# A spacing memset on GpSimd behind the gathers of the last sequence

## The reference

```python
x = L0_attn_x                                        # (8, 512, 128) float32
x = x + 0.5 * ffn(layernorm(x), gate_w, w1, w3, w2)  # 8 experts, each token goes to 2 of them
x = x + attn(layernorm(x), ...)                      # scan over the tokens of a sequence
x = x + 0.5 * ffn(layernorm(x), gate_w, w1, w3, w2)  # the same experts again

def ffn(x, gate_w, w1, w3, w2):
    probs = softmax(x @ gate_w)
    weights, experts = top_k(probs, 2)               # weights divided by their sum
    # out[token] = sum over its 2 experts of weight * (silu(x @ w1[e]) * (x @ w3[e])) @ w2[e]
```

## Time and profile before

| | us |
|---|---|
| time, median of 3 runs | 606.3 |
| lowest and highest of the 3 | 605.97, 606.87 |
| the profiled execution's own time | 611.62 |
| span of the profiled execution, from the first to the last instruction | 609.8 |
| PE busy in it | 525.3 |
| DVE busy | 438.5 |
| POOL busy | 398.1 |
| ACT busy | 318.7 |

### The profile page before, as it was taken

How to read it: one execution, slowest core, us unless ns; L and a number is a source line. 1 busy time by engine, 2 the same in 40 slices (tenths; PEclk the granted TensorE clock), 3 DMA queues, 4 the chain that set the end, 5 groups by cost and what they waited for, 6 DMA issues and landing times.

```text
span 609.8 us, 18683 instructions
## 1 busy us (share of the span) xinstructions
PE 525.3 (86%) x5906; PEld 480.7 (79%) x5906; DVE 438.5 (72%) x1241; ACT 318.7 (52%) x703; POOL 398.1 (65%) x500
## 2 busy tenths in 40 slices
PE   1234899999999899999989989999999999998992
PEld 1233789998977789778888779898798988998981
DVE  4871873556778998879999885887888857248742
ACT  5433574444675657576375663587456454443420
POOL 1182049499999991199954999300985997999982
PEclk9999899999999999999999998999999999999997
DMA  8963233445332221222221132210112432523322
GB/s 278 330 210 110 60 102 110 131 145 128 90 98 83 72 79 55 69 62 66 83 76 49 59 114 75 67 42 27 54 59 84 113 107 76 182 81 102 97 71 60
DMA packets 88632, 60.28 MB, mean 99 GB/s; under 512 B 10337, under 2 KB 82146, under 8 KB 88418
## 3 DMA queue, kind: packets, MB, share of 16 engines
q1 hardware_dynamic: 55586, 31.03, 17.3%
q0 software_dynamic: 8192, 16.79, 9.6%
q10 hardware_dynamic: 24768, 11.28, 6.4%
HBM read 29.69 MB, written 29.37 MB: 97 GB/s over the span
## 4 chain that ended last, share of the span: by engine, by line
PE 61%; issue 10%; ACT 9%; DVE 8%; SPq 5%; POOL 4%; DMA 1%; another core or an unknown queue 1%; DVEq 0%; ACTq 0%; POOLq 0%
PE py L1330 20%; PE pa L1316 16%; PE pb L1316 15%; PE pT L1303 3%; POOL rows_in L766 3%; PE bkB L1380 2%; ACT xn L866 2%; PE bkB L1401 2%; DVE h L1170 1%; ACT sil L847 1%; POOL pace L801 1%; SPq L664 1%; PE bkA L1380 1%; SPq L677 1%
## 5 line engine op out<-in xcount | busy, mean ns | idle before, releaser
L766 POOL DMA_INDIRECT rows_in<-parts,slot x128 | 135.2, 1057 | 179.5 <-DVE slot L1091 157.6
L1330 PE MATMUL py<-ffn_w,h 128*128 x1416 | 196.6, 282 | 9.5 <-ACT yrow L830 8.1
L1170 DVE TENSOR_TENSOR h<-sil,pb 128x512 f32<-128x512 f32 x177 | 120.8, 686 | 107.1 <-PE pb L1316 56.3
L1330 PEld LDWEIGHTS py<-ffn_w,h 128*128 128x128 f32 x1416 | 173.2, 193 | 15.1 <-issue 12.3
L1316 PE MATMUL pa<-rT,ffn_w 128*128 128x128 f16 (+1 forms) x1752 | 150.9, 232 | 18.1 <-DVE h L1170 9.8
L1316 PE MATMUL pb<-rT,ffn_w 128*128 128x128 f16 (+1 forms) x1752 | 155.8, 231 | 0.0
L1316 PEld LDWEIGHTS pa<-rT,ffn_w 128*128 x1752 | 123.3, 99 | 33.4 <-issue 21.8
L785 POOL DMA_INDIRECT yg<-rows_out,slot x120 | 121.0, 1008 | 19.4 <-issue 19.2
L801 POOL MEMSET pace<- 128x544 uint8 x232 | 133.0, 573 | 0.2
L1316 PEld LDWEIGHTS pb<-rT,ffn_w 128*128 x1752 | 122.9, 98 | 7.5 <-issue 0.2
L847 ACT ACTIVATE sil<-pa 128x512 f32<-128x512 f32 x177 | 105.4, 595 | 37.8 <-PE pa L1316 32.3
(11 more groups left out here) (167 smaller groups left out, 493.5 us busy)
## 6 DMA issues: line engine op xcount, KB each, us to landing
rows_out<-yrow ACTq DMA_DIRECT2D x162, 64.0 KB
rin<-rows_in SPq DMA_DIRECT2D x65, 128.0 KB
rows_in<-zrow SPq DMA_DIRECT2D x34, 128.0 KB
shared<-in_w SPq DMA_DIRECT2D x16, 256.0 KB, 6.8
rin<-rows_in SPq DMA_DIRECT2D x47, 64.0 KB
rows_in<-zrow SPq DMA_DIRECT2D x2, 1472.0 KB, 12.1
xres<-in_x SPq DMA_DIRECT2D x4, 512.0 KB, 5.8
ffn_w<-in_w SPq DMA_DIRECT2D x8, 256.0 KB
```

Of the source, the lines that this page charges most:

```text
L766: pool.indirect_dma_start(rows_in[g][:], bass.IndirectOffsetOnAxis(ap=slot[:, c, at:at + 1], axis=0), parts[:, at, :], None).then_inc(s_sc ...
L1170: dve.tensor_tensor(h[:, t % RING, :], sil[:, t % 2, :], pb[t % 2][:], ALU.mult).then_inc(s_h, 1)
L1330: mm = pe.matmul(py[:], h[:, step % RING, at:at + T], w, start=(c == 0), stop=(c == FC - 1))
```

## The change

The condition `t < TILES - 1` is taken away, and the loop over the last run's gathers gets the same memset behind each gather but the very last one, with the count of `sent` carried on.

```diff
@@ -796,12 +796,15 @@
                     scatter(*one)
                 else:
                     gather(*one)
-                if t < TILES - 1:
-                    wait(pool, s_pace, sent - PACES + 1)
-                    pool.memset(pace[:, sent % PACES, :], 0).then_inc(s_pace, 1)
+                wait(pool, s_pace, sent - PACES + 1)
+                pool.memset(pace[:, sent % PACES, :], 0).then_inc(s_pace, 1)
             for run in range(RUNS):
                 for one in every(run, range(UNITS[run] if PEND[run] == TILES else 0)):
                     gather(*one)
+                    sent += 1
+                    if one != (run, UNITS[run] - 1, JU - 1, TOPK - 1):
+                        wait(pool, s_pace, sent - PACES + 1)
+                        pool.memset(pace[:, sent % PACES, :], 0).then_inc(s_pace, 1)
```

## The result

The changed kernel takes 609.61 us in the median of five runs (609.04 to 609.86), the kernel before on the same chip 606.87 (605.97 to 607.89). The ratio is 1.0046, with a 95% interval of 1.0034 to 1.0059, which is 2.1 to 3.6 us slower. The forecast was 609.3 and slower. The kernel before is at 606.87 here and not at the 606.3 of three runs from which the forecast started, so the addition is 2.7 to 2.8 us where 3.0 was forecast.

A forecast was written before the change was run, and what follows sets the result against it. The prediction took GpSimd's queue and its closing DRAIN to set the kernel's end. Seven memsets at 0.43 us add 3.0 us, nothing hidden, to the runs' median: 606.3 + 3.0 = 609.3 us, range 606.0 to 610.2.

The forecast's parts named there:

- The DRAIN as the last to end: At the closing barrier, line 452: GpSimd's DRAIN ends last, at 609.6 us, 2.5 us after the output is complete.
- 0.43 us for each memset, 3.0 in all: GpSimd's last eight gathers: a gather with memset takes 1.69 us instead of 1.256; seven memsets cost 3.0 us.
- the bound of 3.6: Upper bound in us for the seven memsets, from the mean of 37 earlier gathers with memsets, some of them slow.
- The tail of 9.2 us that moves along: GpSimd's DRAIN ends 9.2 us behind the last gather and keeps that distance, so the barrier moves by 3.0 us.
- The rival with the shrinking tail: GpSimd's DRAIN clears what bare gathers left; memset pauses shorten it, halved to 4.6 us gives 604.7 us; chance 0.08.
- the one whose tail doesn't follow: GpSimd's DRAIN end stays at 609.6 us whatever the last gather does; time 606.3 to 607.1 us; chance 0.24.
- The output's end: VectorE's last add and SyncE's last transfer: complete 0.8 us later, at 607.9 instead of 607.1, 4.7 ahead of GpSimd.
- The late rows: TensorE's last rows, which held VectorE until 602.20 us in the earlier trace and left the last gathers 2.25 us spare.
- the 4 us in the earlier trace: Unexplained time between TensorE's last rows of tile 176, over at 595.9, and ScalarE's copy at 599.88; perhaps missing in other executions.
- The lead of 2.5 us for GpSimd: In the profile of the kernel before, GpSimd's end at 609.6 us is 2.5 us later than the output's at 607.1.
- The adds of VectorE beside the memsets: Eight closing adds that may run while GpSimd writes zeros: at most 0.3 us slower, taken as nothing.
- From the start of a gather to its use: Time from a gather's start until VectorE can use its data: 2.7 us, read off the second of the last gathers.

The follow-up runs named there:

- before once more: The kernel before, unedited, timed against itself and profiled a second time: ratio 0.9987.
- 8 bare: The kernel before with the memsets behind the last 8 of the 232 listed transfers taken away as well: ratio 1.0156, 9.5 us slower.
- three quarters: The kernel before with memsets of three quarters of the width behind the last 24 listed transfers, none between the last eight gathers: ratio 1.0034, 2.1 us slower.
- 24 bare: The kernel before with the memsets behind the last 24 of the 232 listed transfers taken away as well: ratio 1.0441, 27 us slower.
- half width with a bare end: The kernel before with half-width memsets behind the last 12 listed transfers, none between the last eight gathers: ratio 1.0113, 6.9 us slower.

## Why the prediction was right, and where it was not

**The DRAIN as the last to end: right.** It was read off against the chain of the page. Of the eleven further profiles, six have GpSimd's DRAIN end 3.0 us or more behind SyncE's, both of the changed kernel among them; in three the two meet within 0.2 us (before once more, 8 bare, three quarters), and in two (24 bare, and half width with a bare end) the output is last.

**0.43 us for each memset, 3.0 in all: right.** 0.42 each and 2.95 in all; the runs gave 2.8 and, when repeated on another chip, 3.5. None of the slow gathers that made the bound of 3.6 fell among the eight.

**The tail of 9.2 us that moves along: right, and now shown.** Its end is 9.2 to 9.3 us behind the last instruction of the queue in every profile of this study, bare gathers or not, and also behind memsets that did nothing. The rival with the shrinking tail is out, as is the one whose tail doesn't follow.

**The output's end: right in its number. The late rows: wrong.** The output was to come 0.8 us later, and counted from the first of the eight gathers it came 0.7 later. It was complete at 602.8 us, 4.7 ahead of the end of GpSimd's DRAIN at 607.5, as forecast. Both numbers go by the last gather, which holds VectorE in the forecast as in the trace, so the late rows don't enter them. The late rows themselves I had wrong. I kept them where they were, and took the 4 us in the earlier trace rows for something that might be missing in other executions. They are there in the second profile of the kernel before and missing in the changed kernel, because of the change: the copy of the last rows comes 5.3 us behind the start of the first gather instead of 9.3, and VectorE waited 2.3 us for the last gathers where I had 0.8. The step that failed is that the added memsets act on GpSimd's own queue alone; bare gathers were taken to cost the other engines nothing. It did no harm to the forecast, because GpSimd's end is the last and the late rows hold neither end after the change.

**The lead of 2.5 us for GpSimd: of one execution.** The second profile of the kernel before has none, 607.2 against 607.3. There too nearly the whole 3.0 falls on GpSimd's end. Had the output been late by more, part of the 3.0 would have been hidden, and the profile on which I worked couldn't have told.

**The adds of VectorE beside the memsets: right at nothing.** They take 0.74 us in pairs in after, and 0.73 or 0.74 before.

**From the start of a gather to its use:** 2.7 us was taken from the second gather; the last one of after has 600.00 - 597.34 = 2.66. The estimate of 2.15 us by the Trainium skill ("DMA: Bandwidth & Descriptors", the section on the anatomy of one DMA on the GpSimd path) is 0.5 short of both rows, and the measurement decides.

## What to carry to other kernels

Look at what each engine does at the closing barrier before you believe the chain that ended last: the DRAIN of GpSimd ends 9.2 us behind the last instruction of its queue here, so its last work has to be over well before that of the others, and what is added between or behind the last transfers is paid nearly in full. Elsewhere in the same queue the pause is worth its price: without the last 8 of the list the kernel is 9.5 us slower, although by their price in the queue they would take 3.4. An idle time with an unnamed releaser is a question to settle by an experiment, not an accident to discount.

## What the runs showed of the hardware

TensorE, or the word of what it has done, is held up by GpSimd's gathers when they follow each other too closely. Starts 1.256 us apart stop it once three to six have begun (three with 8 bare transfers, six in the last stretch with 24), until about the last of them or up to 2 us behind it. 1.45 us apart hold it up in part in the list, and not between the last eight gathers; 1.57 us leaves small waits; at 1.68 us none are seen in this stretch. VectorE's and ScalarE's own instructions take their usual time meanwhile (0.69 us for the product `h`, 0.28 for a copy of `yrow`); what comes late is what they need of TensorE. The multiplications that stop wait for nothing in the program: they come singly, with 0.3 to 1.2 us between them.

It isn't so for all indirect transfers. The 16 scatters at the start of every kernel are bare as well, and most start 1.26 or 1.27 us apart. In the kernel before six of them have begun by 34.91 us, with more to follow, and TensorE multiplies then and ScalarE takes the result up 0.04 us after it is done on record:

```profile
34.91 1.09 PE L1395 MATMUL bkA<-ident,xn 128*128 128x128 f32 x4 [11.55 <-ACT xn L866]
36.04 0.60 ACT L884 ACTIVATE xnT<-bkA 128x512 f32<-128x512 f32 x1 [1.27 <-issue]
```

TensorE has only 24 multiplications in that stretch, from 27 to 50 us. Whether the direction of the transfers or its light load spares it was not tried.

What in TensorE is starved (its instructions, its weights, or the reports of its completion) was not tried and stays open. In 570 to 583 us of the kernel with 24 bare transfers the DMA engines were busy for 31% of the time in the mean, less than the 49% before the stop, so their mean load doesn't explain it. The queues that bring instructions have no packet on record in those 13 us; whether as cause or consequence, the trace doesn't say. Nor was a pause tried in which GpSimd does nothing, so that it is the distance of the transfers and not the memset that helps is argued from the widths, not shown.

GpSimd's closing DRAIN ends 9.2 us behind its last instruction, whether this is a transfer or a memset. What it does in that time stays open as well.
